# A result's row as 2*token + choice: one VectorE instruction in place of a VectorE and a GpSimd one, and the GpSimd tile program written out

## What is computed

```python
h = tokens(x)                                  # [128, 65, 128]
h = h + lstm(layernorm(h))
xt = layernorm(h).reshape(-1, 128)             # 8320 tokens
probs = softmax(xt @ router_w.T + router_b)
topk_p, topk_i = top_k(probs, 2)
gates = sum(onehot(topk_i, 16) * topk_p[..., None], axis=1)
for e in range(16):
    y = gelu(xt @ w1[e].T + b1[e]) @ w2[e].T + b2[e]
    acc = acc + y * gates[:, e:e + 1]
h = h + acc
```

## Time and profile before

| | |
|---|---|
| median of 3 runs | 864.33 us (863.94 to 864.53) |
| profiled execution, span from first to last instruction | 863.2 us |
| busy TensorE / weight loads | 667.7 (77%) / 623.5 (72%) us |
| busy VectorE | 609.5 (71%) us |
| busy ScalarE | 424.3 (49%) us |
| busy GpSimd | 535.0 (62%) us |
| DMA | 140.77 MB, mean 163 GB/s |

### The profile page before, as it was taken

How to read it: one execution, slowest core, us unless ns; L and a number is a source line. 1 busy time by engine, 2 the same in 40 slices (tenths; PEclk the granted TensorE clock), 3 DMA queues, 4 the chain that set the end, 5 groups by cost and what they waited for, 6 DMA issues and landing times. The chain is left out here.

```text
span 863.2 us, 27254 instructions
## 1 busy us (share of the span) xinstructions
PE 667.7 (77%) x7853; PEld 623.5 (72%) x7854; DVE 609.5 (71%) x1896; ACT 424.3 (49%) x1206; POOL 535.0 (62%) x653
## 2 busy tenths in 40 slices
PE   3999996988979979979995128888888888888500
PEld 3999996988969969969994017777767777776500
DVE  3689995986868959958987507666666666666478
ACT  3456563564555536545564117555555555555200
POOL 0123663764746637647667636888888888888800
PEclk9999997998989989989998559999999999999855
DMA  8767674774765757748730343333233332222187
GB/s 315 261 215 247 224 257 155 228 249 158 236 211 194 236 152 257 238 152 266 227 119 29 89 110 79 90 88 83 82 85 85 86 83 84 83 84 75 18 302 291
DMA packets 73858, 140.77 MB, mean 163 GB/s; under 512 B 13430, under 2 KB 55874, under 8 KB 65470
## 3 DMA queue, kind: packets, MB, share of 16 engines
q1 hardware_dynamic: 62992, 120.43, 43.8%
q0 software_dynamic: 9280, 17.21, 6.0%
q10 hardware_dynamic: 1518, 2.41, 1.1%
HBM read 116.29 MB, written 25.66 MB: 164 GB/s over the span
## 5 line engine op out<-in xcount | busy, mean ns | idle before, releaser
L950 POOL DMA_INDIRECT back<-patches x160 | 189.7, 1186 | 39.8 <-issue 36.6
L973 PE MATMUL bank<-ws,patches 128*128 128x128 f32 (+1 forms) x1408 | 182.0, 288 | 9.5 <-DMA patches<-in_x 9.5
L973 PEld LDWEIGHTS bank<-ws,patches 128*128 128x128 f32 (+1 forms) x1408 | 172.9, 202 | 9.2 <-ACT whi L449 9.2
L541 ACT ACTIVATE patches<-bank,b1s 128x256 f32<-128x256 f32 x320 | 125.4, 475 | 92.2 <-PE bank L1076 92.2
L922 POOL DMA_INDIRECT sent<-pay,slot_own x130 | 147.2, 1132 | 34.6 <-issue 34.0
L898 POOL TENSOR_TENSOR rstd<-veps,cst 128x2 f32<-128x2 f32 (+1 forms) x68 | 48.5, 714 | 149.3 <-DVE veps L624 148.5
L1076 PE MATMUL bank<-patches,ex_hi 128*128 128x256 f16 x640 | 111.1, 276 | 16.4 <-issue 15.2
L1088 PE MATMUL bank<-ex_hi,patches 128*128 x1280 | 112.9, 221 | 3.6 <-DVE patches L857 3.5
L840 DVE TENSOR_SCALAR patches<-patches 128x2 int32<-128x2 f32 x80 | 21.1, 264 | 115.3 <-DMA back<-patches 98.3
L857 DVE TENSOR_TENSOR patches<-patches 128x1024 f16<-128x1024 f32 x80 | 98.0, 1225 | 2.8
L973 PE MATMUL bank<-whi,xhi 128*128 128x128 f16 x512 | 90.3, 221 | 4.7 <-DVE xlo L659 4.7
(11 more groups left out here) (130 smaller groups left out, 1578.0 us busy)
## 6 DMA issues: line engine op xcount, KB each, us to landing
patches<-in_x SPq DMA_DIRECT2D x64, 1152.0 KB
patches<-sent SPq DMA_DIRECT2D x80, 130.0 KB
patches<-back SPq DMA_DIRECT2D x26, 320.0 KB, 4.8
ex_raw<-in_we SPq DMA_DIRECT2D x64, 128.0 KB
b2r<-in_b SPq DMA_DIRECT2D x80, 64.0 KB, 2.9
posr<-in_pos SPq DMA_DIRECT2D x65, 64.0 KB
out_tower<-h SPq DMA_DIRECT2D x13, 320.0 KB, 4.3
back<-patches POOLq DMA_INDIRECT x160
```

Of the source, the lines that this page charges most:

```text
L541: last = act.activation(hf[n.mod(2)][:, c * ROWS:(c + 1) * ROWS], ps_up(n, c), ACT.Gelu, bias=b1s[:, bass.ds(e * FC + c, 1)], scale=1.0 / ...
L950: pool.indirect_dma_start(back, bass.IndirectOffsetOnAxis(ap=dsti[q][:, k:k + 1], axis=0), yo[q][:, k, :], None, bounds_check=2 * TOKENS - ...
L973: last = pe.matmul(bank_of, l, w_, start=(c == KS and k == 0), stop=(c == KS - 1 and k == 2))
```

## The change

`tag` holds 2 * token as a float. VectorE computes the row of `back` in one instruction, (first choice != expert) + 2 * token, and writes it as an integer to `dsti`. `dsto`, GpSimd's addition and the semaphores `dst_a` and `dst_b` are gone, and `dst_done` takes the place of `dst_b`. GpSimd's program of the expert stage is written out as 82 single steps, so that all of its waits are against constants. In `back` the two results of a token lie beside each other, so one load brings both choices of 5 positions.

```diff
--- before.py
+++ after.py
@@ -54,7 +54,7 @@
 NPOS = 4
 NY = 8
 PACK, SEND = 5, 10
-NO_TOKEN = 1 << 20
+NO_ROW = float(1 << 20)
 CT = 5
 
 
@@ -70,7 +70,7 @@
     c[:, C_ONE:C_IOTA] = 1.0
     c[:, C_IOTA:C_EBASE] = np.tile(np.arange(E), UG)
     c[:, C_EBASE:C_TOK] = np.arange(E) * CAP
-    c[:, C_TOK:C_BSC] = T * np.arange(P)[:, None] + np.arange(T)
+    c[:, C_TOK:C_BSC] = 2 * (T * np.arange(P)[:, None] + np.arange(T))
     c[:, C_POW] = -0.5
     c[:, C_BSC:C_POW] = [0.5, 0.5, 1.0, 0.5]
     c[:, C_J] = ROWS * np.arange(P)
@@ -200,7 +200,6 @@
             return arena[:, used[0] - words:used[0]]
 
         xt = [part(HALVES * ROW).rearrange("p (a w) -> p a w", a=HALVES) for _ in range(4)]
-        dsto = [part(HALVES).bitcast(I32) for _ in range(4)]
         dsti = [part(HALVES).bitcast(I32) for _ in range(4)]
         tabj = part(2 * TILES_B).rearrange("p (a j) -> p a j", a=2)
         yo = [part(HALVES * HID).rearrange("p (a h) -> p a h", a=HALVES) for _ in range(4)]
@@ -260,7 +259,7 @@
         in_ps, in_done = sem("in_ps"), sem("in_done")
         up_ps, gelu_done, hhi_done, hlo_done = sem("up_ps"), sem("gelu_done"), sem("hhi_done"), sem("hlo_done")
         down_ps, y_done = sem("down_ps"), sem("y_done")
-        tagged, dst_a, dst_b = sem("tagged"), sem("dst_a"), sem("dst_b")
+        tagged, dst_done = sem("tagged"), sem("dst_done")
         y_out = [sem(f"y_out{i}") for i in range(4)]
 
         bk_in = [sem(f"bk_in{i}") for i in range(NX)]
@@ -397,7 +396,7 @@
                 if j.within(0, TILES_B - 1):
                     if j.reg is not None or j.at >= 4:
                         through(sp, in_ps, j - 4)
-                        through(sp, dst_b, j - 4)
+                        through(sp, dst_done, j - 4)
                     row = sp.value_load(tabi[0:1, 1, bass.ds(j.val(), 1)], min_val=0, max_val=E * CAP)
                     sp.dma_start(xt[j.mod(4)], rows_of(sent, row)).then_inc(xt_in[j.mod(4)], 16)
                 j = n + 1
@@ -420,10 +419,8 @@
                 q = m % NX
                 if m >= NX:
                     sp.wait_ge(add_b, (m - NX + 1) * CT)
-                for k in range(2):
-                    sp.dma_start(bk[q][:, k * CT:(k + 1) * CT, :],
-                                 back[k * TOKENS:(k + 1) * TOKENS, :].rearrange("(b t) h -> b t h", t=T)
-                                 [:, m * CT:(m + 1) * CT, :]).then_inc(bk_in[q], 16)
+                sp.dma_start(bk[q], back.rearrange("(b r) h -> b r h", r=2 * T)
+                             [:, m * 2 * CT:(m + 1) * 2 * CT, :]).then_inc(bk_in[q], 16)
 
             for m in range(NX):
                 load(m)
@@ -556,7 +553,7 @@
 
             dve.memset(pad[:, :, :], 0.0).then_inc(setup_dve, 1)
             dve.wait_ge(setup_dve, 1)
-            dve.memset(pad[:, :, HID:HID + 1].bitcast(I32), NO_TOKEN)
+            dve.memset(pad[:, :, HID:HID + 1], NO_ROW)
             dve.wait_ge(setup_act, 2)
 
             dve.scalar_tensor_tensor(wlo[:, :, :].rearrange("p a b -> p (a b)"),
@@ -565,7 +562,7 @@
                                      ALU.subtract).then_inc(setup_dve, 1)
             dve.wait_ge(const_in, 16 * N_CONST)
             dve.tensor_copy(count[:, :], cst[:, C_EBASE:C_TOK])
-            dve.tensor_copy(tag[:, :, 0].bitcast(I32), cst[:, C_TOK:C_BSC])
+            dve.tensor_copy(tag[:, :, 0], cst[:, C_TOK:C_BSC])
             dve.tensor_tensor(lbias[:, 2, :], lbias[:, 0, :], lbias[:, 1, :], ALU.add).then_inc(setup_dve, 1)
             dve.wait_ge(setup_dve, 3)
             dve.tensor_tensor(lbias[:, 2, :], lbias[:, 2, :], cst[:, C_BSC:C_POW], ALU.mult).then_inc(setup_dve, 1)
@@ -837,8 +834,8 @@
                     if n.reg is not None or n.at >= 4:
                         dve.wait_ge(y_out[q], n.div(4) * 16 * HALVES)
 
-                    dve.tensor_scalar(dsto[q], xt[q][:, :, HID + 1], tabj[:, 0, bass.ds(n.val(), 1)],
-                                      float(TOKENS), ALU.not_equal, ALU.mult).then_inc(dst_a, 1)
+                    dve.scalar_tensor_tensor(dsti[q], xt[q][:, :, HID + 1], tabj[:, 0, bass.ds(n.val(), 1)],
+                                             xt[q][:, :, HID], ALU.not_equal, ALU.add).then_inc(dst_done, 1)
                 j = n - 2
                 if j.within(0, TILES_B - 1):
                     q = j.mod(4)
@@ -860,13 +857,13 @@
 
             for m in range(T // CT):
                 q = m % NX
-                dve.wait_ge(bk_in[q], 32 * (m // NX + 1))
+                dve.wait_ge(bk_in[q], 16 * (m // NX + 1))
                 for k, s in ((0, add_a), (1, add_b)):
                     for i in range(CT):
                         t = m * CT + i
                         if k == 1:
                             dve.wait_ge(add_a, t + 1)
-                        dve.scalar_tensor_tensor(h1[:, t, :], bk[q][:, k * CT + i, :], gates[:, k, t:t + 1],
+                        dve.scalar_tensor_tensor(h1[:, t, :], bk[q][:, 2 * i + k, :], gates[:, k, t:t + 1],
                                                  h1[:, t, :], ALU.mult, ALU.add).then_inc(s, 1)
 
         @block.gpsimd
@@ -935,16 +932,9 @@
 
             def step_b(n):
                 j = n - 2
-                sends = j.within(0, TILES_B - 1)
-                if sends:
-                    through(pool, dst_b, j)
+                if j.within(0, TILES_B - 1):
+                    through(pool, dst_done, j)
                     through(pool, y_done, j)
-                if n.within(0, TILES_B - 1):
-
-                    through(pool, dst_a, n)
-                    q = n.mod(4)
-                    pool.tensor_tensor(dsti[q], dsto[q], xt[q][:, :, HID].bitcast(I32), ALU.add).then_inc(dst_b, 1)
-                if sends:
                     q = j.mod(4)
                     for k in range(HALVES):
                         pool.indirect_dma_start(back, bass.IndirectOffsetOnAxis(ap=dsti[q][:, k:k + 1], axis=0),
@@ -952,7 +942,8 @@
                                                 oob_is_err=False).then_inc(y_out[q], 16)
 
             pool.wait_ge(plan_done, 1)
-            slots_b(pool, step_b, 6, TILES_B - 1)
+            for n in range(TILES_B + 2):
+                step_b(At(None, n, UB))
 
         @block.tensor
         def _(pe):
```

## The result

The change makes the kernel slower: 885.03 us (878.22 to 887.96, 4 runs) against 864.13, a ratio of 1.023 [1.018, 1.029]. Forecast were 799.1 us and a range of 793 to 826. The same two kernels side by side in two later series gave 1.011 [1.006, 1.017] and 1.016 [1.009, 1.023], and in a third the changed kernel took 849.3, 881.6, 886.5 and 886.7 us. The ratios leave out runs of over 1.5% above a kernel's fastest, so where a kernel's runs fall into two groups all of them are named here.

A forecast was written before the change was run, and what follows sets the result against it. GpSimd's queue, in turns with store landings, was taken as the bound. Tiles at 2.93 instead of 3.71 us, a shorter backlog and final stage took 65.2 us off the 863.2 us span; adding 1.1 gave 799.1, range 793 to 826.

The forecast's parts named there:

- What bounds the kernel now: Expert stage, 3.71 us per tile: GpSimd's queue and the landing of stores take turns as last; TensorE needs 2.87.
- Part 1: GpSimd's L946 addition goes: 62.5 us less busy time, and stores of n-2 no longer wait for L840 of n.
- D: Start of VectorE's destination instruction in tile n; D+3.27 is 3.27 us later, the forecast end of the second store.
- Part 2: VectorE's L840 becomes one scalar_tensor_tensor on 128x2: between -0.02 and +0.18 us per tile, taken as 0.
- Part 4: GpSimd's written-out program removes register arithmetic; the gap between stores stays 0.30 us, so taken as 0.
- Part 5: Setup before the expert stage: tag and pad get floats instead of integers, cost 0.
- Part 3: SyncE's slot wait ends with L840 instead of L946: next x load issued 2.2 us earlier, nobody's wait longer.
- Part 6: Final stage, one load of 10 contiguous rows per partition instead of two of 5: -0.3 us, bounds -0.7 and +0.5.
- The cycle after: Expert stage after the change: the return of a stored tile is late next, 2.93 us per tile, just above TensorE's 2.87.
- the store loses twice: Rival: the first store doesn't slip in between cast and subtraction, 3.56 us per tile, time 849 us; chance 0.07.
- The sum: Whole kernel: 61.4 us from the tiles, 3.5 from the end backlog, 0.3 from the final stage, 65.2 us less.
- The slower rival: GpSimd's written-out instructions arrive late: slower from a stall of 1.2 us per step, 972 us at 2.58; chance 0.04.

The follow-up runs named there:

- e5: The kernel before with eight slots instead of four for the destination rows, and VectorE's wait for stores moved to tile n-6's, before the output: 817.39 us, 0.947.
- e9: The changed kernel with SyncE's x tile load also waiting for VectorE's subtraction, some 2.2 us later, no GpSimd work added: 856.9 us, ratio 0.988.
- e1: The kernel before with only GpSimd's tile program written out: 864.24 us, ratio 0.9995.
- e3: The changed kernel plus an unused GpSimd addition of 128x2 constants before the stores: 11 runs, five of 860.9 to 865.9 us, six of 871.7 to 889.9.

## Why the prediction was wrong, point by point

- **What bounds the kernel now** failed first. TensorE's 2.87 us were right (2.86 with eight slots), and that the waits for landing and GpSimd's queue "take turns" was on the page. But I gave the weight to GpSimd. With the landing alone moved off the path (e5) the kernel before gains 5.3% at the same work on GpSimd.
- **Part 1**, the addition: right in sign. With the load kept late it gains 1.2% (e9), some 9 us, and not 61. What held the addition up, VectorE's subtraction, now holds the store that took its place: before, the first store ended 3.61 us after the destination instruction (641.30 to 644.91), after the change it would end at D+3.27.
- **Part 2**, the new VectorE instruction: 219 ns measured against 0.23 us assumed, 0 was right. **Part 4**: 0, right (e1). **Part 5** has no run of its own; the first output came 0.91 us later, less than such starts differ between the runs.
- **Part 3** is the step that decides the sign: "After, it can be issued 2.2 us earlier. Nobody's wait gets longer." The timing was right, the conclusion wrong. The earlier load costs 3% (e9 against the changed kernel). The late x tile had, in the place read in e9, kept TensorE, and through it VectorE, from taking two tiles without a pause.
- **Part 6**: -0.3 forecast, +0.23 measured before the adds, within the bounds.
- **The cycle after**. Two terms of it were wrong, and one was right. First, the start of a store behind L847 is 0.83 us, not 0.13. The row that I took the earlier trace rows was misread. GpSimd's order around it is, from the kernel before:

```profile
650.13 0.56 POOL L946 TENSOR_TENSOR patches<-patches 128x2 int32<-128x2 int32 x1
650.84 1.93 POOL L950 DMA_INDIRECT back<-patches  x1
...
654.39 0.46 POOL L946 TENSOR_TENSOR patches<-patches 128x2 int32<-128x2 int32 x1
655.00 0.99 POOL L950 DMA_INDIRECT back<-patches  x1 [0.15 <-issue]
```

  Each step is an addition and then two stores, so the store at 653.07 is the second of its tile. It waits for no output; it follows the first one by 0.30 us. The output that ends at 652.94 belongs to the next tile, whose first store starts at 655.00. Counted with its own output, no first store of the kernel before starts less than 0.85 us after it, so the right number was in the trace. With it the first store begins in the subtraction and not in the cast, and whether it slips in between never came up. Put in alone, this term gives the 3.56 us per tile of the rival "the store loses twice", which would still be faster than before. Second, I set the tiles evenly apart. The chain through two tiles fixes only the sum of two distances; the profiled run had 2.33 + 5.86, and in that division the second tile's cast and subtraction lie over the first tile's stores, 2.21 + 0.30 + 1.69 instead of the 2.58 that I had from D+0.69 to D+3.27. The landing was right: 2.60 us in the rows shown, 2.58 taken.
- **The sum**: 79 times 0.78 us were to be saved, 79 times 0.16 were lost. The backlog at the end shrank by 0.9 and not by 3.5: the last outputs come 2.3 to 2.9 us apart, and GpSimd is still behind them.
- **The rivals**. "The store loses twice" is the nearest, with 3.56 us per tile against 3.87 (4.1 in pairs), and had 0.07. Its own condition, stores that are held once by each of VectorE's long instructions, did come about, by the late start. The slower rival, late instructions, was given 0.04 and did not happen; what happened wasn't among the four. What the Trainium skill, SBUF — State Buffer, section SBUF: two separate sides, says of the exclusive lock is borne out for waiting: a store begun in the two-input subtraction ended 0.85 us after it. But a whole-instruction lock it is not in these rows: a store that is once under way goes on beside a subtraction that starts meanwhile, as in the earlier trace rows, and is held again only by a cast.

**What stays open.** How a late x tile opens pairs is read from one place of one trace. The run of the changed kernel at 849 us and those of e3 at 861 to 866 us have no profile, so what their tiles did isn't known. Why some runs have long stretches without pairs and others none isn't known either. The kernel before with the early load wasn't tried, since the addition reads the x slot that the load overwrites; e3 stands in for it.

## What to carry to other kernels

Where a loop waits for something of four steps ago, write down two steps' chain with the two placed close together as well as evenly apart, and look which of them renews itself; an average rate hides it. A wait that is moved to an earlier release can take away what spaced the engines, so its gain is not bounded by zero from below. And ask first what the longest wait protects: here it was two numbers per partition, and eight slots for them were worth 5.3% to the kernel before and 7.3% together with the change, which alone cost 1 to 2%.

## What the runs showed of the hardware

- The first indirect store of a tile starts 0.83 us or more after the end of the VectorE instruction that it waits for; this is the least in all 16 profiles, and it is 0.83 to 0.87 us where GpSimd had been idle in the changed kernel. Behind GpSimd's own last instruction a store starts 0.30 us or more after a store and 0.15 us or more after an addition.
- A store alone takes 0.97 to 0.99 us in most cases. Begun inside a cast or a two-input subtraction of VectorE it ends 0.83 to 0.89 us after it in nearly all cases of the 16 profiles, or later if the next cast holds it once more.
- A cast that starts 0.17 to 0.53 us into a store holds it: the store ends 0.12 us after the cast. One that starts later doesn't; up to some 0.8 us into the store it is itself lengthened, in the kernel before to as much as 0.94 us instead of 0.68:

```profile
649.70 0.94 DVE L855 CAST patches<-patches 128x1024 f16<-128x1024 f32 x1
```

- One and the same program, the changed kernel, took 849 us and 887 us in turns on the same chip.
